# Single tiles of the first expert layer: tokens as the stationary operand, weights as the moving one, and the hidden rows turned back

## The chip, the cores and the metric

The kernel runs on one core of a Trainium2 chip. The metric is the device time of one execution in microseconds (us), the median of three runs. A core has a matrix engine (PE; its weight loads are listed apart, as PEld), a vector engine (DVE), a scalar engine (ACT), a general engine (POOL), which here also issues the indirect transfers, and a queue engine (SP) for plain transfers. A matrix instruction multiplies a stationary operand of 128 x 128, loaded by a weight load ahead of it, with a moving operand of 128 rows and up to 512 columns, and sums into PSUM, which has eight banks of 128 x 512 float32.

## What is computed

Sixteen images and sixteen texts become 165 tokens of 256 numbers each. Two layers follow, each of attention or a scan and then experts. The change lies in the experts of the first layer:

```python
macro_scores = jax.nn.sigmoid(xf @ macro_w)          # 4 groups, the best one is taken
micro_scores = jax.nn.sigmoid(jnp.einsum('td,gde->tge', xf, micro_w))   # both experts of the group
w = (macro_full[:, :, None] * micro_full).reshape(T, NUM_EXPERTS)
gate = jax.nn.silu(jnp.einsum('td,edf->tef', xf, gate_w))   # 256 -> 512
up = jnp.einsum('td,edf->tef', xf, up_w)
h = gate * up
out = jnp.einsum('te,tef,efd->td', w, h, down_w)            # 512 -> 256
```

Each token goes to one group of four, and through both experts of that group. The kernel computes these products in pairs of float16: an operand is split into a high and a low half, and three products (high x high, high x low, low x high) stand for one in float32.

## The kernel before

Tokens are sorted by group into 24 tiles of 128 rows (`SLOT0`). The first 20 tiles form ten pairs, worked on two at a time, with 256 token columns; the last four are worked on singly (`SINGLES0 = 4`), with 128. A pair or a single is a unit: units 0 to 9 are pairs, 10 to 13 singles. `pipelined` (L145) writes units 0 and 1, a hardware loop over units 2 to 7, and then units 8 to 13 one by one. A function of this kind writes each engine's own list of steps; each engine runs its list strictly in order, and semaphores hold it where it needs another engine.

On PE, `tile` (L861) writes for each unit: the products of the unit's first expert (`products_in`, s = 0, in two halves of 256 hidden columns), the transposes of the next unit's token rows (`transpose_x`), the output product of the unit before through its second expert (`product_out(i - 1, 1)`), the products of the second expert (s = 1), and the output product of the first (`product_out(i, 0)`). In `products_in` (L839) a 128 x 128 piece of the weights is stationary and the tokens, held transposed, move; so the hidden rows come out with the hidden index on the partitions, which is what `product_out` (L852) needs for its stationary operand. Its moving operand is 256 columns of the output weights. For a single tile `products_in` issues 24 matrix instructions of 128 columns for a half, 96 for a unit, and `product_out` 12 of 256 columns for an expert. The expert's place in the weights is a register value, read at the start of each unit by `weights` (L857).

Between them ACT applies Silu to the gate (L906) and writes the high half of the scaled hidden rows (L911), and DVE multiplies by `up` (L955) and writes the low half (L960). This goes in four steps per unit, `b` = 0 to 3. The input products use PSUM banks 0 to 3, the outputs banks 4 and 5 (`Y_BANKS`), the token transposes bank 7. ACT then scales the first expert's output (`first_y`, L919), DVE adds the second's (`whole_y`, L969), and POOL sends the rows with an indirect transfer that adds to a sum in device memory (L1017). When all are sent, SP loads that sum back (L1258), DVE takes its statistics, and the attention of the second layer begins; PE meanwhile prepares that layer's routing weights (`prepare_logits`, L1484 and after), and fills waits there with idle products on ones (`keep_clock`, L550).

Far ahead of this, SP loads the expert weights in twelve pieces (L1996), the first ten with a semaphore each and the last two with one between them, and ACT and POOL split them (L2185, L2050).

Of the kernel before, what the change touches and what calls it, by code (L numbers as in the profile page):

```python
# [17 lines left out]
P = 128  # L18
# [116 lines left out]

C_BANKS = (0, 1)
Y_BANKS = (4, 5)

def tile_rows(t):
# [16 lines left out]
def known(i, value):  # L158

    return isinstance(i, int) and i == value  # L160
# [18 lines left out]
def build(nc, txt, patches, wtok, cols, rows_a, consts, pe_table, wsmall, w0, wattn, rows_f, w1, wsmall1,  # L179
          b2rows, out):  # L180
    with ExitStack() as ctx:
# [3 lines left out]
        def sem(name):  # L185
            return ctx.enter_context(nc.semaphore(name))
# [206 lines left out]
        d_moved = sem("d_moved")  # L393
        own_high = sem("own_high")
        w0_split = sem("w0_split")
        w0_loaded = [sem(f"w0_loaded{i}") for i in range(XW // CW // 2 - 1)]

        def w0_landed(m):

            last = len(w0_loaded) - 1  # L400
            return (w0_loaded[m], 16) if m < last else (w0_loaded[last], 32)
        consts_ready = sem("consts_ready")
        rows_known = sem("rows_known")
        dve_done = sem("dve_done")
# [37 lines left out]
        act_out = sem("act_out")  # L442
        h_ready = sem("h_ready")
        y_half = sem("y_half")
        hT_hi = sem("hT_hi")
        hT_lo = sem("hT_lo")
        y_done = sem("y_done")
# [206 lines left out]
        def moved0(slot, tiles):  # L654

            return 16 * len([t for t in range(tiles) if unit0(t) % 2 == slot])

        def landed0(i, slot, j):
            return moved0(slot, first0(i) + 1) if single0(i) else 32 * (j + 1)

# [155 lines left out]
        def pe_experts0(pe):  # L816
            def transpose_x(i, slot, j):
                pe.wait_ge(x_in[slot], landed0(i, slot, j))
                for k in range(KC):
                    for a in range(tiles0(i)):  # L820
                        ins = nc.tensor.transpose(PS[:, 7, (2 * k + a) * P:(2 * k + a + 1) * P],  # L821
                                                  xin[:, slot, a, k * P:(k + 1) * P], k_ident)
                ins.then_inc(x_tr, 1)

            def products_in(i, s, half, w_, slot):

                b = 2 * s + half
                if b == 0:
                    pe.wait_ge(x_lo, i + 1)
                if not (known(i, 0) and s == 0):  # L830
                    pe.wait_ge(h_ready, 4 * i + b - 1)
                tokens = P * tiles0(i)
                for u, done in ((0, gate_psum), (1, up_psum)):
                    for c in range(2):
                        n = 0
                        for k in range(KC):
                            off = in_w0(s * W0N + (u * KC + k) * F0 + (2 * half + c) * P)
                            for x_, at_ in ((xh, off), (xl, off), (xh, off + CW)):
                                ins = nc.tensor.matmul(PS[:, 2 * u + half, c * T1:c * T1 + tokens], w_[:, at_:at_ + P],  # L839
                                                       x_[:, slot, k, 0:tokens], start=(n == 0), stop=(n == 3 * KC - 1))  # L840
                                n += 1
                    ins.then_inc(done, 1)

            def product_out(i, s, w_):

                pe.wait_ge(hT_lo, 4 * i + 2 * s + 2)
                wait_from(pe, y_copied if s else y_begun, first0(i))
                for a in range(tiles0(i)):
                    for c in range(F0 // P):
                        off = in_w0(s * W0N + 2 * KC * F0 + c * D)  # L850
                        for n, (h_, at_) in enumerate(((hTh, off), (hTh, off + CW), (hTl, off))):
                            ins = nc.tensor.matmul(PS[:, Y_BANKS[s], a * D:(a + 1) * D], h_[:, s, c, a * P:(a + 1) * P],  # L852
                                                   w_[:, at_:at_ + D], start=(c == 0 and n == 0),
                                                   stop=(c == F0 // P - 1 and n == 2))
                ins.then_inc(y_done if s else y_half, 1)

            def weights(i):  # L857
                return expert_weights(w0x, 2 * E0 * W0N, slot_expert(pe, first0(i), G0))
            held = [None, None]

            def tile(i, slot, j):  # L861
                w_ = weights(i)
                if known(i, 0):
                    transpose_x(0, 0, 0)
                    keep_clock(18, 6)
                products_in(i, 0, 0, w_, slot)
                products_in(i, 0, 1, w_, slot)
                if not known(i, 0):

                    last = held[1] if slot == 1 or isinstance(i, int) and held[0] == i - 1 else weights(i - 1)  # L870
                if not known(i, UNITS0 - 1):
                    transpose_x(i + 1, 1 - slot, j + slot)
                if not known(i, 0):
                    product_out(i - 1, 1, last)
                products_in(i, 1, 0, w_, slot)
                products_in(i, 1, 1, w_, slot)
                product_out(i, 0, w_)
                held[:] = [i if isinstance(i, int) else None, w_]
            pipelined(pe, UNITS0, tile, SINGLES0)
            product_out(UNITS0 - 1, 1, weights(UNITS0 - 1))  # L880

        def x0_parts(i, half, slot):

# [3 lines left out]

        def h0_parts(i, b):

            s, half = b // 2, b % 2  # L890
            views = (PS[:, half, :].rearrange("p (c r) -> p c r", c=2), PS[:, 2 + half, :].rearrange("p (c r) -> p c r", c=2),
                     sg[:, half], hh[:, half], hTh[:, s, 2 * half:2 * half + 2], hTl[:, s, 2 * half:2 * half + 2])
            if single0(i):
                return (v[:, :, 0:P] for v in views)
            return (v.rearrange("p c r -> p (c r)") for v in views)

        def act_experts0(act):
# [3 lines left out]
                nc.scalar.activation(to, from_, ACT.Copy).then_inc(x_hi, 1)  # L901

            def nonlinear(i, b):
                act.wait_ge(gate_psum, 4 * i + b + 1)
                gate, _, to, _, _, _ = h0_parts(i, b)
                nc.scalar.activation(to, gate, ACT.Silu).then_inc(act_out, 1)  # L906

            def split_h(i, b):
                act.wait_ge(h_ready, 4 * i + b + 1)
                _, _, _, whole, to, _ = h0_parts(i, b)  # L910
                nc.scalar.activation(to, whole, ACT.Copy, scale=hscale[:, 0:1]).then_inc(hT_hi, 1)  # L911

            def first_y(i, slot, j):
# [4 lines left out]
                for a in range(tiles0(i)):  # L918
                    nc.scalar.activation(ybuf[:, slot, a, :], PS[:, Y_BANKS[0], a * D:(a + 1) * D], ACT.Copy,  # L919
                                         scale=wall[:, bass.ds(first0(i) + a, 1), 0]).then_inc(y_begun, 1)  # L920

            def tile(i, slot, j):
                if known(i, 0):
                    split_x(0, 0)
                    act.wait_ge(scale_ready, 1)
                else:
                    first_y(i - 1, 1 - slot, j + slot - 1)
                for b in range(4):
                    nonlinear(i, b)
                    split_h(i, b)  # L930
                    if b == 1 and not known(i, UNITS0 - 1):
                        split_x(i + 1, 1 - slot)
            pipelined(act, UNITS0, tile, SINGLES0)
            first_y(UNITS0 - 1, (UNITS0 - 1) % 2, (UNITS0 - 1) // 2)

        def dve_experts0(dve, chain):
# [12 lines left out]

            def combine(i, b):  # L950

                dve.wait_ge(up_psum, 4 * i + b + 1)
                dve.wait_ge(act_out, 4 * i + b + 1)
                _, up, gate, whole, _, _ = h0_parts(i, b)
                nc.vector.tensor_tensor(whole, up, gate, ALU.mult).then_inc(h_ready, 1)  # L955

            def split_h(i, b):
                dve.wait_ge(hT_hi, 4 * i + b + 1)
                _, _, _, whole, high, low = h0_parts(i, b)
                nc.vector.scalar_tensor_tensor(out=low, in0=whole, scalar=hscale[:, 0:1], in1=high, op0=ALU.mult,  # L960
                                               op1=ALU.subtract).then_inc(hT_lo, 1)

            def whole_y(i, slot):

                dve.wait_ge(y_done, i + 1)
                for a in range(tiles0(i)):
# [3 lines left out]
                                                   scalar=wall[:, bass.ds(first0(i) + a, 1), 1], in1=part, op0=ALU.mult,  # L970
                                                   op1=ALU.add).then_inc(y_copied, 1)

            def tile(i, slot, j):
                if known(i, 0):
                    split_x(0, 0)
                    row_weights(0, 0, 0)
                for b in range(4):
                    combine(i, b)
                    split_h(i, b)
                    if b == 1:  # L980
                        if not known(i, UNITS0 - 1):
                            split_x(i + 1, 1 - slot)
                            row_weights(i + 1, 1 - slot, j + slot)
                        if not known(i, 0):
                            whole_y(i - 1, 1 - slot)
            pipelined(dve, UNITS0, tile, SINGLES0)
            whole_y(UNITS0 - 1, (UNITS0 - 1) % 2)

        def pool_slots(pool, tiles, lag, gather, send):
# [1731 lines left out]
```

## Time and profile before

| | |
|---|---|
| three runs, median (lowest to highest) | 790.91 us (790.46 to 791.1) |
| profiled execution, its own time | 791.43 us |
| its span, first to last instruction | 789.6 us |
| PE busy | 719.4 us, 91% of the span |
| DVE, ACT, POOL busy | 468.2, 375.5, 356.6 us |
| mean granted clock of PE | 0.966 |

The first expert layer runs from about 146 to 352 us of the span, its four single units from about 305 us. In the timeline each line is a run of like instructions on one engine: its start, how long it lasted, engine, line of the kernel, operation, output and inputs, and the count after an x; a bracket at the end is the idle time ahead of it and what ended it. Since matrix instructions overlap, the distance from the start of one group to the start of the next on PE tells what the group took of PE.

### The profile page before, as it was taken

The numbers are of one execution on the slowest core, as the hardware profiler recorded it, in microseconds if no ns is written. First come the engines' busy times: TensorE is split into PE (matmuls) and PEld (weight loads), VectorE is DVE, ScalarE is ACT, GpSimd is POOL, SyncE is SP. The second block draws the span as 40 slices with busy tenths as digits, with TensorE's granted clock in tenths as the row PEclk, the third lists the DMA queues.
The fourth block names the chain that finished last, engine by engine and source line by source line (L and its number), as shares of the span: only waits on it lengthen the run. The fifth ranks groups of instructions, "written<-read, shape, count | busy, mean of one in ns | idle before, by whom it ended". The sixth has DMA issues, their size and how long they took to land.

```text
span 789.6 us, 19052 instructions
## 1 busy us (share of the span) xinstructions
PE 719.4 (91%) x6285; PEld 632.7 (80%) x6286; DVE 468.2 (59%) x1241; ACT 375.5 (48%) x887; POOL 356.6 (45%) x310
## 2 busy tenths in 40 slices
PE   5989983899999999998798997989999999999991
PEld 4768973888888898778688986868888888888871
DVE  4998678444444444337888888945455454554540
ACT  5797657343333343334465665533444434434430
POOL 2539980322233223211676871043665555655331
PEclk9999995999999999999999999999999999999996
DMA  9970044114122111117121334411322233222225
GB/s 270 411 306 2 1 148 148 49 28 117 28 32 41 33 22 29 22 21 226 57 81 54 85 97 159 145 52 38 55 44 47 43 54 54 46 48 41 40 35 150
DMA packets 37192, 66.25 MB, mean 84 GB/s; under 512 B 3776, under 2 KB 29360, under 8 KB 35568
## 3 DMA queue, kind: packets, MB, share of 16 engines
q1 hardware_dynamic: 23696, 46.90, 17.7%
q0 software_dynamic: 13248, 18.21, 14.4%
q8 instruction: 37, 0.61, 0.3%
q10 hardware_dynamic: 192, 0.38, 0.1%
q14 instruction: 19, 0.16, 0.1%
HBM read 44.83 MB, written 23.35 MB: 86 GB/s over the span
## 4 chain that ended last, share of the span: by engine, by line
PE 67%; DVE 15%; POOL 8%; DMA 3%; ACT 3%; issue 2%; POOLq 0%; SPq 0%; DVEq 0%; ACTq 0%
PE PS L839 17%; PE PS L1046 15%; PE PS L1059 15%; PE PS L852 8%; POOL X L2050 6%; PE PS L1419 3%; PE PS L1446 1%; PE PS L1031 1%; DMA Y<-in_wtok_dram 1%; PE PS L1427 1%; POOL X L1671 1%; POOL X L2045 1%; PE PS L821 1%; DVE stats L2467 1%; DVE rs L2400 1%
## 5 line engine op out<-in xcount | busy, mean ns | idle before, releaser
L839 PE MATMUL PS<-Y,X 128*128 128x256 f16 (+1 forms) x1344 | 139.0, 258 | 1.6 <-issue 0.9
L839 PEld LDWEIGHTS PS<-Y,X 128*128 x1344 | 119.4, 98 | 18.2 <-issue 3.1
L1225 POOL DMA_INDIRECT sum<-X,dest x45 | 88.8, 1973 | 96.6 <-ACT X L1128 81.4
L1059 PE MATMUL PS<-X 128*128 x720 | 125.7, 273 | 2.0 <-ACT X L1128 1.9
L1046 PE MATMUL PS<-X 128*128 128x256 f16 (+1 forms) x768 | 122.6, 265 | 0.4 <-issue 0.4
L1118 ACT ACTIVATE X<-PS,X 128x256 f32<-128x256 f32 (+1 forms) x192 | 72.6, 461 | 103.3 <-PE PS L1046 100.2
L1046 PE MATMUL PS<-X,Y 128*128 128x256 f16 (+1 forms) x384 | 100.2, 264 | 0.0
L1059 PE MATMUL PS<-Y,X 128*128 x360 | 98.2, 273 | 0.0
L1017 POOL DMA_INDIRECT sum<-Y,dest x24 | 38.7, 1611 | 116.1 <-DVE Y L969 112.8
L1046 PEld LDWEIGHTS PS<-X 128*128 x768 | 71.8, 97 | 10.3 <-issue 0.9
L1059 PEld LDWEIGHTS PS<-X 128*128 128x128 f16 x720 | 70.4, 98 | 11.1 <-issue 3.1
L955 DVE TENSOR_TENSOR Y<-PS,Y 128x512 f32<-128x512 f32 (+1 forms) x56 | 34.4, 615 | 68.8 <-PE PS L839 65.2
L1211 POOL DMA_INDIRECT X<-xs,source x45 | 45.7, 1015 | 65.2 <-DVE source L750 33.0
L911 ACT ACTIVATE Y<-Y,hscale 128x512 f16<-128x512 f32 (+1 forms) x56 | 37.0, 660 | 72.3 <-DVE Y L955 72.3
L852 PE MATMUL PS<-X,Y 128*128 x576 | 67.6, 273 | 0.4 <-DVE Y L960 0.3
L1177 DVE SCALAR_TENSOR_TENSOR PS<-PS,hscale,X 128x256 f32<-128x256 f32 x45 | 20.0, 488 | 74.8 <-PE PS L1059 74.8
L960 DVE SCALAR_TENSOR_TENSOR Y<-Y,hscale 128x512 f16<-128x512 f32 (+1 forms) x56 | 38.1, 680 | 40.8 <-ACT Y L911 40.8
L852 PEld LDWEIGHTS PS<-X,Y 128*128 128x128 f16 x576 | 55.6, 98 | 7.9 <-issue 0.8
L1169 DVE SCALAR_TENSOR_TENSOR X<-X,hscale 128x1024 f16<-128x1024 f32 (+1 forms) x48 | 58.5, 1218 | 1.7
L2050 POOL TENSOR_TENSOR X<-X 128x256 f16<-128x256 f32 (+1 forms) x55 | 58.2, 1092 | 0.5
L1007 POOL DMA_INDIRECT Y<-xs,source x24 | 23.7, 989 | 59.4 <-DVE Y L947 29.8
L906 ACT ACTIVATE Y<-PS 128x512 f32<-128x512 f32 (+1 forms) x56 | 29.6, 528 | 32.9 <-PE PS L839 32.4
(402 smaller groups left out, 1389.6 us busy)
## 6 DMA issues: line engine op xcount, KB each, us to landing
X<-in_w_dram SPq DMA_DIRECT2D x11, 1024.0 KB, 16.1
stage<-in_w_dram SPq DMA_DIRECT2D x16, 512.0 KB, 3.5
sum<-h SPq DMA_DIRECT2D x2, 2048.0 KB, 7.5
xs<-Y SPq DMA_DIRECT2D x2, 1040.0 KB, 5.4
xs<-Y SPq DMA_DIRECT2D x2, 1032.0 KB, 5.1
h<-in_txt_dram SPq DMA_DIRECT2D x2, 1024.0 KB, 17.3
Y<-in_patches_dram SPq DMA_DIRECT2D x3, 672.0 KB, 8.2
sum<-h SPq DMA_DIRECT2D x2, 768.0 KB, 6.4
```

Of the source, the lines that this page charges most:

```text
L839: ins = nc.tensor.matmul(PS[:, 2 * u + half, c * T1:c * T1 + tokens], w_[:, at_:at_ + P], x_[:, slot, k, 0:tokens], start=(n == 0), stop=( ...
L852: ins = nc.tensor.matmul(PS[:, Y_BANKS[s], a * D:(a + 1) * D], h_[:, s, c, a * P:(a + 1) * P], w_[:, at_:at_ + D], start=(c == 0 and n == ...
L911: nc.scalar.activation(to, whole, ACT.Copy, scale=hscale[:, 0:1]).then_inc(hT_hi, 1)
L960: nc.vector.scalar_tensor_tensor(out=low, in0=whole, scalar=hscale[:, 0:1], in1=high, op0=ALU.mult, op1=ALU.subtract).then_inc(hT_lo, 1)
L1017: nc.gpsimd.indirect_dma_start(out=sum0, out_offset=bass.IndirectOffsetOnAxis(ap=dest[:, i:i + 1], axis=0), in_=ybuf[:, u % 2, i - first0( ...
L1046: ins = nc.tensor.matmul(PS[:, 2 * s + c // 2, (c % 2) * T1:(c % 2) * T1 + tokens], part[:, off:off + P], x_[:, slot, k, 0:tokens], start= ...
L1059: ins = nc.tensor.matmul(PS[:, 4 + a, 0:D], h_[:, s, c, a * P:(a + 1) * P], part[:, off:off + D], start=(s == 0 and c == 0 and n == 0), st ...
L1118: ins = nc.scalar.activation(hh1[:, s, c, 0:tokens], PS[:, 2 * s + c // 2, (c % 2) * T1:(c % 2) * T1 + tokens], ACT.Gelu, bias=bias1[:, sl ...
L1169: nc.vector.scalar_tensor_tensor(out=lo_, in0=act_, scalar=hscale[:, 2:3], in1=hi_, op0=ALU.mult, op1=ALU.subtract).then_inc(h1_lo, 1)
L1211: nc.gpsimd.indirect_dma_start(out=x1in[:, u % 2, n - first_tile(u), :], out_offset=None, in_=xs1, in_offset=bass.IndirectOffsetOnAxis(ap= ...
L1225: nc.gpsimd.indirect_dma_start(out=sum1, out_offset=bass.IndirectOffsetOnAxis(ap=dest[:, i:i + 1], axis=0), in_=y1buf[:, u % 2, i - first_ ...
L2050: ins = nc.gpsimd.tensor_tensor(w0_low(n)[:, of], w0_landing(n)[:, of], w0_high(n)[:, of], ALU.subtract)
```

## The change

Pairs are left as they are. In a single unit the operands of the input products change places: a 128 x 128 piece of the tokens is stationary, and 512 columns of weights move, so one instruction fills a whole bank with the gate (or up) rows of one expert. That makes 12 instructions for an expert and 24 for a unit, in place of 96. The hidden rows now come out with the tokens on the partitions, and Silu and the product with `up` run on 128 x 512 in one step per expert instead of two of 128 x 256. They then have to be turned back: `transpose_h` sends four 128 x 128 float32 transposes through PE into one further bank (`TURN_BANK = 6`), from which ACT and DVE write the high and the low halves. That bank is held until DVE has written the low half. The order in a single unit is written anew on PE, ACT and DVE; `product_out(i, 0)` moves from the end of unit `i` into the next unit, and the last unit's rest follows behind the loop. One semaphore is added for the turned rows, and one is taken from the weight loads, so that the last three pieces share one and all three must land before any of them is split.

```diff
-Y_BANKS = (4, 5)
+Y_BANKS, TURN_BANK = (4, 5), 6
...
-        w0_loaded = [sem(f"w0_loaded{i}") for i in range(XW // CW // 2 - 1)]
+        w0_loaded = [sem(f"w0_loaded{i}") for i in range(XW // CW // 2 - 2)]
...
-            return (w0_loaded[m], 16) if m < last else (w0_loaded[last], 32)
+            return (w0_loaded[m], 16) if m < last else (w0_loaded[last], 48)
...
+            def single_in(i, s, w_, slot):
+                if s == 0:
+                    pe.wait_ge(x_lo, i + 1)
+                pe.wait_ge(h_ready, step0(i, s) - 2)
+                for u, done in ((0, gate_psum), (1, up_psum)):
+                    n = 0
+                    for k in range(KC):
+                        off = in_w0(s * W0N + (u * KC + k) * F0)
+                        for x_, at_ in ((xh, off), (xh, off + CW), (xl, off)):
+                            ins = nc.tensor.matmul(PS[:, 2 * u + s, 0:F0], x_[:, slot, k, 0:P], w_[:, at_:at_ + F0],
+                                                   start=(n == 0), stop=(n == 3 * KC - 1))
+                            n += 1
+                    ins.then_inc(done, 1)
+            def transpose_h(i, s):
+                pe.wait_ge(h_ready, step0(i, s))
+                pe.wait_ge(hT_lo, step0(i, s) - 1)
+                for c in range(F0 // P):
+                    ins = nc.tensor.transpose(PS[:, TURN_BANK, c * P:(c + 1) * P],
+                                              hh[:, s].rearrange("p c r -> p (c r)")[:, c * P:(c + 1) * P], k_ident)
+                ins.then_inc(hT_psum, 1)
...
             def product_out(i, s, w_):
-                pe.wait_ge(hT_lo, 4 * i + 2 * s + 2)
+                pe.wait_ge(hT_lo, step0(i, s) if single0(i) else step0(i, 2 * s + 1))
...
+            def single(i, slot, j):                       # PE
+                w_ = weights(i)
+                after = single0(i - 1)
+                single_in(i, 0, w_, slot)
+                if after:
+                    transpose_h(i - 1, 1)
+                if not known(i, UNITS0 - 1):
+                    transpose_x(i + 1, 1 - slot, j + slot)
+                product_out(i - 1, 0 if after else 1, held[1])
+                single_in(i, 1, w_, slot)
+                transpose_h(i, 0)
+                if after:
+                    product_out(i - 1, 1, held[1])
+                held[:] = [i, w_]
...
-            product_out(UNITS0 - 1, 1, weights(UNITS0 - 1))
+            product_out(UNITS0 - 1, 0, held[1])
+            transpose_h(UNITS0 - 1, 1)
+            product_out(UNITS0 - 1, 1, held[1])
...
+            def single(i, slot, j):                       # ACT
+                after = single0(i - 1)
+                if not after:
+                    first_y(i - 1, 1 - slot, j + slot - 1)
+                nonlinear(i, 0)
+                if after:
+                    split_h(i - 1, 1)
+                if not known(i, UNITS0 - 1):
+                    split_x(i + 1, 1 - slot)
+                if after:
+                    first_y(i - 1, 1 - slot, j + slot - 1)
+                nonlinear(i, 1)
+                split_h(i, 0)
...
+            split_h(UNITS0 - 1, 1)
             first_y(UNITS0 - 1, (UNITS0 - 1) % 2, (UNITS0 - 1) // 2)
...
+            def single(i, slot, j):                       # DVE
+                after = single0(i - 1)
+                combine(i, 0)
+                if after:
+                    split_h(i - 1, 1)
+                if not known(i, UNITS0 - 1):
+                    split_x(i + 1, 1 - slot)
+                    row_weights(i + 1, 1 - slot, j + slot)
+                if not after:
+                    whole_y(i - 1, 1 - slot)
+                combine(i, 1)
+                split_h(i, 0)
+                if after:
+                    whole_y(i - 1, 1 - slot)
...
+            split_h(UNITS0 - 1, 1)
             whole_y(UNITS0 - 1, (UNITS0 - 1) % 2)
```

## Rows read from the trace of the kernel before

**Rows 1.** The page's part 4: the chain that ended last, by engine.
```profile
PE 67%; DVE 15%; POOL 8%; DMA 3%; ACT 3%; issue 2%; POOLq 0%; SPq 0%; DVEq 0%; ACTq 0%
```

**Rows 2.** The chain in order of time: start us, us, what held the end.
```profile
297.20 5.24 PE PS L839 x48
...
351.58 0.50 DVE Y L969
...
352.34 4.49 DMA sum<-Y,dest
...
356.89 2.86 DMA h<-sum
...
363.19 0.34 DVE X L1717
```

**Rows 3.** Timeline of PE over the single units and what follows.
```profile
304.90 3.20 PE L839 MATMUL PS<-Y,X 128*128 128x128 f16 x48
307.94 0.39 PE L821 MATMUL PS<-cst,Y 128*128 128x128 f32 x2
308.16 2.78 PE L852 MATMUL PS<-X,Y 128*128 x24
...
315.45 4.29 PE L839 MATMUL PS<-Y,X 128*128 128x128 f16 x48 [0.31 <-issue]
...
321.15 3.96 PE L839 MATMUL PS<-Y,X 128*128 128x128 f16 x48
325.15 1.50 PE L852 MATMUL PS<-X,Y 128*128 x12
326.91 4.45 PE L839 MATMUL PS<-Y,X 128*128 128x128 f16 x48 [0.26 <-issue]
...
350.04 1.50 PE L852 MATMUL PS<-X,Y 128*128 x12 [0.33 <-DVE Y L960]
351.38 1.04 PE L1484 MATMUL PS<-cst,Y 128*128 128x128 f32 x8
352.34 1.05 PE L1488 MATMUL PS<-onesf,wsm 1*128 1x1 f32 x8
```

**Rows 4.** PE groups by form: busy us, mean ns of one; idle before.
```profile
L839 PE MATMUL PS<-Y,X 128*128 128x128 f16 x384 | 30.9, 223 | 1.1 <-issue 0.9
```

**Rows 5.** Last weight load's issue, landing times of all twelve, a late split on ACT.
```profile
46.62 0.43 SPq L1996 DMA_DIRECT2D stage<-in_w_dram  x1
...
DMA to landing us min/median/max: 5.3/15.1/26.1
...
101.45 1.06 ACT L2185 ACTIVATE X<-X 128x1024 f16<-128x1024 f32 x1 [0.30 <-POOL X L2050]
```

**Rows 6.** DVE and ACT on 128 x 512, by form, and two DVE starts.
```profile
L955 DVE TENSOR_TENSOR Y<-PS,Y 128x512 f32<-128x512 f32 x40 | 27.6, 691 | 51.9 <-PE PS L839 48.3 <-ACT Y L906 3.6
L960 DVE SCALAR_TENSOR_TENSOR Y<-Y,hscale 128x512 f16<-128x512 f32 x40 | 30.4, 759 | 31.6 <-ACT Y L911 31.6
L901 ACT ACTIVATE Y<-PS 128x512 f16<-128x512 f32 x10 | 5.8, 579 | 9.6 <-PE PS L821 9.6
...
299.86 0.69 DVE L955 TENSOR_TENSOR Y<-PS,Y 128x512 f32<-128x512 f32 x1 [1.74 <-PE PS L839]
349.25 0.49 DVE L960 SCALAR_TENSOR_TENSOR Y<-Y,hscale 128x256 f16<-128x256 f32 x1 [0.58 <-ACT Y L911]
```

**Rows 7.** PE after idle time, and a stretch with its granted clock (PEclk).
```profile
52.75 1.37 PE L2295 MATMUL PS<-cst,Y 128*128 128x128 f32 x8 [1.39 <-DVE Y L2513]
357.82 2.02 PE L1502 MATMUL PS<-Y,X 128*128 128x260 f32 x8 [1.08 <-ACT wsm L1617]
363.66 0.66 PE L1390 MATMUL PS<-cst,X 128*128 128x128 f32 x2 [0.93 <-DVE X L1717]
...
391.37 0.69 PE L1407 MATMUL PS<-cst,X 128*128 128x128 f32 x2 [3.43 <-ACT X L2074]
...
core 0: us, PE busy (x), PEclk, DMA share, GB/s
52.00:54.00 2.00, 1.14 (x9) 1.00 1.05 442
364.00:366.00 2.00, 2.00 (x14) 0.50 0.98 330
```

More of the change, by code:

```diff
@@ L444, in build @@
         y_half = sem("y_half")
+        hT_psum = sem("hT_psum")
         hT_hi = sem("hT_hi")
@@ L656, in moved0, with step0, alone0 @@
             return 16 * len([t for t in range(tiles) if unit0(t) % 2 == slot])
+        def step0(i, b):
+            return 4 * PAIRS0 + 2 * (i - PAIRS0) + b + 1 if single0(i) else 4 * i + b + 1
+        def alone0(i, s):
+            return 2 * (i - PAIRS0) + s + 1
         def landed0(i, slot, j):
@@ L859, in pe_experts0 @@
             held = [None, None]
+            def single(i, slot, j):
[12 more added lines that the diff above has]
+                held[:] = [i, w_]
             def tile(i, slot, j):
+                if single0(i):
+                    single(i, slot, j)
+                    return
                 w_ = weights(i)
@@ L888, in h0_parts @@
         def h0_parts(i, b):
+            if single0(i):
+                turned = PS[:, TURN_BANK, :].rearrange("p (c r) -> p c r", c=F0 // P)
+                return (PS[:, b, :], PS[:, 2 + b, :], sg[:, b].rearrange("p c r -> p (c r)"), hh[:, b].rearrange("p c r -> p (c r)"),
+                        turned, hTh[:, b, :, 0:P], hTl[:, b, :, 0:P])
             s, half = b // 2, b % 2
             views = (PS[:, half, :].rearrange("p (c r) -> p c r", c=2), PS[:, 2 + half, :].rearrange("p (c r) -> p c r", c=2),
-                     sg[:, half], hh[:, half], hTh[:, s, 2 * half:2 * half + 2], hTl[:, s, 2 * half:2 * half + 2])
-            if single0(i):
-                return (v[:, :, 0:P] for v in views)
+                     sg[:, half], hh[:, half], hh[:, half], hTh[:, s, 2 * half:2 * half + 2], hTl[:, s, 2 * half:2 * half + 2])
             return (v.rearrange("p c r -> p (c r)") for v in views)
@@ L903, in nonlinear @@
             def nonlinear(i, b):
-                act.wait_ge(gate_psum, 4 * i + b + 1)
-                gate, _, to, _, _, _ = h0_parts(i, b)
+                act.wait_ge(gate_psum, step0(i, b))
+                gate, _, to, _, _, _, _ = h0_parts(i, b)
                 nc.scalar.activation(to, gate, ACT.Silu).then_inc(act_out, 1)
             def split_h(i, b):
-                act.wait_ge(h_ready, 4 * i + b + 1)
-                _, _, _, whole, to, _ = h0_parts(i, b)
+                if single0(i):
+                    act.wait_ge(hT_psum, alone0(i, b))
+                else:
+                    act.wait_ge(h_ready, step0(i, b))
+                _, _, _, _, whole, to, _ = h0_parts(i, b)
                 nc.scalar.activation(to, whole, ACT.Copy, scale=hscale[:, 0:1]).then_inc(hT_hi, 1)
@@ L920, in first_y @@
                                          scale=wall[:, bass.ds(first0(i) + a, 1), 0]).then_inc(y_begun, 1)
+            def single(i, slot, j):
[11 more added lines that the diff above has]
+                split_h(i, 0)
             def tile(i, slot, j):
+                if single0(i):
+                    single(i, slot, j)
+                    return
                 if known(i, 0):
@@ L950, in combine @@
             def combine(i, b):
-                dve.wait_ge(up_psum, 4 * i + b + 1)
-                dve.wait_ge(act_out, 4 * i + b + 1)
-                _, up, gate, whole, _, _ = h0_parts(i, b)
+                dve.wait_ge(up_psum, step0(i, b))
+                dve.wait_ge(act_out, step0(i, b))
+                _, up, gate, whole, _, _, _ = h0_parts(i, b)
                 nc.vector.tensor_tensor(whole, up, gate, ALU.mult).then_inc(h_ready, 1)
             def split_h(i, b):
-                dve.wait_ge(hT_hi, 4 * i + b + 1)
-                _, _, _, whole, high, low = h0_parts(i, b)
+                dve.wait_ge(hT_hi, step0(i, b))
+                _, _, _, _, whole, high, low = h0_parts(i, b)
                 nc.vector.scalar_tensor_tensor(out=low, in0=whole, scalar=hscale[:, 0:1], in1=high, op0=ALU.mult,
@@ L971, in whole_y @@
                                                    op1=ALU.add).then_inc(y_copied, 1)
+            def single(i, slot, j):
[12 more added lines that the diff above has]
+                    whole_y(i - 1, 1 - slot)
             def tile(i, slot, j):
+                if single0(i):
+                    single(i, slot, j)
+                    return
                 if known(i, 0):
```

## The prediction

> **What bounds the kernel now.** I read the page's part on the chain that ended last first: PE holds 67% of it, no other engine more than 15% [rows 1]. What matters is whether PE holds it where the change is made. The chain in order of time says so: through the expert layer it consists of input products (L839) and output products (L852), one behind the other, without a pause between pairs; behind the last single unit it passes to DVE's last addition, to POOL's last indirect transfer, to SP's load of the sum, and by DVE's norm back to PE [rows 2]. So a microsecond taken from PE before the last output product is a microsecond off the end, as long as nothing on that line is late for a reason of its own, and everything behind it moves along.
>
> Then the timeline of PE. The reader should compare pitches there, that is the distance of group starts over the count, not durations, since instructions overlap. In a pair 48 products of 256 columns take 5.24 us [rows 2], 109 ns each. In the singles 48 products of 128 columns should take half; the first unit comes near that, 48 in 3.04 us (304.90 to 307.94) or 63 ns each. But the next units take 4.00 us (321.15 to 325.15), 83 ns each, and lose more at their starts: 12 output products alone take 1.34 us (350.04 to 351.38), yet the next unit begins 1.76 us after they do (325.15 to 326.91), with idle time that ends by "issue", so with no other engine to blame [rows 3]. A single unit takes 11.46 us (315.45 to 326.91). By columns it should take 96 x 55 ns + 2 x 1.34 + 0.22, some 8.2 us. PE is thus bound by getting its many short instructions and weight loads out, not by columns. All 384 of them are busy for 30.9 us [rows 4].
>
> **The change part by part.** *Input products.* The columns stay: 96 x 128 per unit are now 24 x 512. No 512-column product stands in the trace; the nearest are the float16 products of 256 columns, which also read one operand at a register's address, at 109 ns. Twice that is 218 ns, 2.62 us for the 12 of one expert. Bounds: no gain per column against the singles as they are, 4 x 83 = 333 ns; below, 213 ns, a column per cycle of 2.4 GHz, which 109 ns for 256 columns come close to. I take 218, since only the column count differs. The weight load of the next piece of tokens lies beside 218 ns of streaming, as it does beside 109 in a pair.
>
> The Trainium skill ("TensorE: Matmul & The Clock Gate", Back-to-back issue gap) gives a sustained 131 ns for products of 512 columns with their loads, and 216 alone; the pairs' 109 ns for half the columns speaks for the second. By the first the 96 products would take 8.4 us less than I reckon.
>
> *Turning back.* Eight times four float32 transposes. The trace has the same kind at 0.96 us for 8 (351.38 to 352.34) and 0.22 for 2 [rows 3]: 0.12 each, 0.48 for a turn. Bounds 0.11 and 0.20 (the 0.39 that two last by themselves), that is -0.3 to +2.6 us over 32; I take 0.12, as they follow one another.
>
> *Output products* stay: 1.34 us for 12, 24 x 109 ns = 2.62 for those of the last pair. *Token transposes* stay: 0.22.
>
> *Sum on PE, with nothing late.* Unit 10: 2.62 in + 0.22 + 2.62 out of pair 9 + 2.62 in + 0.48 = 8.56. Units 11 and 12: 2.62 + 0.48 + 0.22 + 1.34 + 2.62 + 0.48 + 1.34 = 9.10 each. So unit 13 begins at 304.90 + 8.56 + 18.20 = 331.66.
>
> *The new waits.* In unit 11 or 12, from its start: input products end at 2.62 and 7.28, turns at 3.10 and 7.76, output products run from 3.32 and 7.76. DVE began 0.20 after the pitch end of its products (297.04 + 2.62 against 299.86); on 128 x 512 DVE takes 0.69 for the product and 0.76 for the low half, ACT 0.58 out of PSUM [rows 6]. So the first expert's hidden rows are there at 3.51 and are turned from 7.28; the rows turned at 3.10 have their low half at about 4.7, and the next turn, which needs their bank, comes at 7.28, their output product at 7.76; the rows turned at 7.76 are split by 9.3, while the next turn is at 11.7 and the output product at 12.4. The smallest margin is over 2 us. PE has behind each of these waits all it has left, so a late split would cost in full, but none is late. ACT waits for the turn with the next tokens' split and the first output behind it; these end at about 5.3, and the next unit's products need the tokens at 9.10. POOL's sends come 9 us apart and land 4.5 us after they start [rows 2], and its gathers need only the token transposes, which stay early.
>
> *The tail is where it costs.* Unit 13 has no token transposes. Its last turn in the loop ends at 7.54 from its start, the output product of unit 12 at 8.88. ACT 7.74 to 8.32, DVE 8.34 to 9.10, and PE starts 0.30 after DVE (349.74 to 350.04, [rows 3, 6]): 9.40, so PE idles 0.5. Output product to 10.74, turn to 11.22, ACT 11.42 to 12.00, DVE 12.02 to 12.78, PE at 13.08 after 1.9 us of waiting with nothing to put there. Before, no turn stood in this line. Last output product: 331.66 + 13.08 = 344.74, against 350.04. The gain is 5.3 us. It would be some 7.7 without the two waits.
>
> *The rest.* The last three weight loads share a semaphore. The last is issued at 46.62 and at the longest landing seen, 26.1 us, is there by 73; the first chunk that newly waits is split on ACT at 101.45, held by POOL [rows 5]. Cost nothing, cover 28 us. The last unit's register load at the end falls away: hidden already.
>
> The profiled execution: 789.6 - 5.3 = 784.3 of span, with the same 1.8 us around it 786.1. The median of the runs lies 0.5 lower than that execution's time, so 790.91 - 5.3 = **785.6 us**. The start gaps of units 11 to 13 (0.42 each, 1.3 us in all) I count as gone, because PE now streams 218 ns per instruction, and the issuing gets ahead as it does in pairs; if they stay, 786.9.
>
> **The rivals.**
> *The tail lets the clock fall.* Idle of 1.39 us (52.75) left the clock at 1.00; 3.43 us ahead of 391.37 and the pair of 1.08 and 0.93 ahead of 363.66 were followed by 0.50, the 1.2 GHz level [rows 7]. The tail has 0.5 and 1.9 within four microseconds, between. Then the last 12 output products take 1.3 us more, and the preparation behind them, at half speed, some 0.3 to 1 more than its cover: 787.2 to 787.9. Against it: dense work just before. A fall that moves behind the layer can also spare the one at 364, up to 2 us the other way.
> The Trainium skill (the same page, PE-mode transpose) says that transposes don't keep the clock up as products do; here four of them stand between 12 products each, and the eight of L1484 ran without a fall.
> *PE waits for the turned rows in each unit*, because ACT or DVE are later than reckoned: from 2 us of lateness on, each step adds. Three units at 1.2 us: 789.2. Against it the margins above.
> *The wide products stream no cheaper* than four short ones: slower. Place: all 96. At 333 ns they cost 96 x 115 = 11.0 us more than reckoned, 796.6. It decides from 218 + 5300/96 = 273 ns on. For it: the singles' own rate per column; against it: the pairs' 109 ns.
> *Wide products overlap*, so that 512 columns take hardly longer than 256. At 109 ns they cost 96 x 109 = 10.5 us less: 775.1. Against it: in the pairs and the first single unit time goes with columns. The Trainium skill's 131 ns above belongs here and would give 777.2.
>
> **How the numbers follow.** Forecast 0.71, with its own range 784.0 to 787.0; clock in the tail 0.14; waits in each unit 0.07; wide products slow 0.06; overlap 0.02. What a measurement here can tell from no change is 0.2%, 1.6 us: 789.3 to 792.5. Faster: 0.71 + 0.14 + 0.02 and half of the waits, 0.90. Same: the other half and a mild case of slow products, 0.05. Slower 0.05. The range runs from 783.0 (the cheapest bounds, -0.8 us, and the fall at 364 spared) to 789.3 (waits), and leaves out the slow products and the overlap.
>
> **What would show it.** In the changed trace 12 products of 512 columns should take 2.6 us by their starts and a unit 9.1; four turns 0.5; PE idle only twice, 0.5 and 1.9 us, ahead of the last two output products; the last of them should begin at about 344.7 and the sum's load at about 351.6. A unit at over 10.5 us with PE idle "DVE L960" says waits; the same without idle says slow products; 0.50 in the clock from 343 to 348 says the tail. If the load of the sum comes 5 us earlier and the end does not, the prediction is wrong behind the layer.

## The result, and the profile after

The changed kernel takes 784.16 us (median of four runs, 783.53 to 784.72) against 791.0 in the same comparison: ratio 0.9913, 95% interval 0.9902 to 0.9925. Forecast were 785.6 and a range of 783.0 to 789.3. The profiled execution took 783.53 us with a span of 781.7; before, 791.43 and 789.6. Now and then a run of a kernel, changed or not, takes some 10 us more than its others.

In the changed kernel's lines, L862 are the wide input products, L872 the turn, L884 the output products, L829 the token transposes, L968 and L1035 the high and low halves on ACT and DVE, L1578 the first step behind the layer. First its timeline of PE (start us, us, engine, line, operands, count, idle before), which answers to [rows 3]:

```profile
303.99 2.75 PE L862 MATMUL PS<-X,Y 128*128 x12
306.58 0.38 PE L829 MATMUL PS<-cst,Y 128*128 128x128 f32 x2
...
312.01 0.60 PE L872 MATMUL PS<-cst,Y 128*128 128x128 f32 x4
312.45 2.75 PE L862 MATMUL PS<-X,Y 128*128 x12
315.04 0.60 PE L872 MATMUL PS<-cst,Y 128*128 128x128 f32 x4
315.47 0.38 PE L829 MATMUL PS<-cst,Y 128*128 128x128 f32 x2
315.69 1.47 PE L884 MATMUL PS<-X,Y 128*128 x12
317.00 2.75 PE L862 MATMUL PS<-X,Y 128*128 x12
319.59 0.60 PE L872 MATMUL PS<-cst,Y 128*128 128x128 f32 x4
320.03 1.47 PE L884 MATMUL PS<-X,Y 128*128 x12
321.34 2.75 PE L862 MATMUL PS<-X,Y 128*128 x12
...
337.59 1.47 PE L884 MATMUL PS<-X,Y 128*128 x12
339.40 1.50 PE L884 MATMUL PS<-X,Y 128*128 x12 [0.34 <-DVE Y L1035]
340.74 0.60 PE L872 MATMUL PS<-cst,Y 128*128 128x128 f32 x4
342.99 1.50 PE L884 MATMUL PS<-X,Y 128*128 x12 [1.65 <-DVE Y L1035]
344.32 1.04 PE L1578 MATMUL PS<-cst,Y 128*128 128x128 f32 x8
```

The reader sees a unit without a bracket, that is without idle time: from 312.45 to 321.34 PE goes from group to group, 8.89 us, where a unit took 11.46 [rows 3]. The starts that had idle time by "issue" have none. Only the last two output products wait, for DVE, 0.34 and 1.65 us. From the start of the singles to the last output product it is 342.99 - 303.99 = 39.00 us; before, 350.04 - 304.90 = 45.14. The change itself gives 6.14 us in this pair of traces.

By form (busy us, mean ns of one | idle before), against the 30.9 us of [rows 4]:

```profile
L862 PE MATMUL PS<-X,Y 128*128 x96 | 22.0, 379 | 0.0
```

The rest of the 7.9 us between the spans is not shown to be of the change's making. The singles begin 0.91 us earlier, and so does the whole layer: its first token transposes start at 143.10 against 144.01. In the profiles of the other runs but one the singles begin anywhere from 303.43 to 304.78. Behind the layer the chain of waits is this (start us, us, what; compare [rows 2]):

```profile
342.99 1.50 PE PS L884 x12
...
350.76 2.76 PE PS L1596 x8
353.52 1.73 PE PS L1599 x4
...
357.00 0.38 ACT wsm L1714
357.38 0.08 ACT wsm L1715
...
357.50 0.44 PE PS L1484 x2
```

Before, it passed over the last transfer, the load of the sum and DVE's norm; now it passes over PE's and ACT's preparation of the routing weights, which has become the later of the two. Two things differ on the way there. The last transfer was quicker, 3.74 us from POOL's start to the next load against 4.55 (from 352.34 to 356.89 in [rows 2]):

```profile
345.28 1.55 POOL L1111 DMA_INDIRECT sum<-Y,dest  x1 [3.80 <-DVE Y L1044]
...
349.02 2.80 SPq L1352 DMA_DIRECT2D h<-sum  x5
```

And the clock fell during the preparation instead of behind it (window, length and PE busy, clock; 0.50 is 1.2 GHz), so that L1596 took 2.76 us against 2.02 before [rows 7], and L1599 1.73 against 1.04:

```profile
core 0: us, PE busy (x), PEclk, DMA share, GB/s
342.00:344.00 2.00, 1.01 (x10) 1.00 0.55 66
352.00:354.00 2.00, 2.00 (x6) 0.50 0.95 257
384.00:386.00 2.00, 1.92 (x12) 1.00 0.00 0
```

It is the clock that made the preparation the later one: in the profiles of the experiments e2, e4 and e7 below the transfer was as quick (3.78 to 3.87 us) and the clock stayed up there, and PE waited for DVE's norm again, by 0.8 us. The third row shows the other side: PE idles 3.42 us ahead of 384.08, as it did 3.43 us ahead of 391.37, but the clock stays up this time. Such falls move attention's length from profile to profile. From the load of the sum to the next layer's first store it was 123.8 us before, 122.9 here, and 122.9 to 124.5 in the profiles of the experiments.

### The profile page after: what moved, and what is told of

The parts are those of the page before. It is cut to its first block, busy times and chain, and to the rows that moved or that the text cites. A ratio compares the mean times of both kernels' runs of the same rounds, so it can differ in the third digit from the quotient of the medians.

```text
span 781.7 us, 18313 instructions
## 1 busy us (share of the span) xinstructions
PE 711.0 (91%) x6029; PEld 619.4 (79%) x6030; DVE 465.2 (60%) x1225; ACT 371.6 (48%) x871; POOL 356.5 (46%) x310
## 4 chain that ended last, share of the span: by engine, by line
PE 67%; DVE 15%; POOL 8%; ACT 4%; issue 2%; DMA 1%; POOLq 0%; SPq 0%; DVEq 0%; ACTq 0%
PE PS L1140 15%; PE PS L1153 15%; PE PS L847 13%; PE PS L884 8%; POOL X L2144 6%; PE PS L1513 3%; PE PS L862 3%; PE PS L1540 1%; PE PS L1125 1%; PE PS L1521 1%; POOL X L2139 1%; POOL X L1765 1%; DMA ccols<-in_cols_dram 1%; PE PS L829 1%; DVE rs L2494 1%
## 5 line engine op out<-in xcount | busy, mean ns | idle before, releaser
L847 PE MATMUL PS<-Y,X 128*128 128x256 f16 x960 | 108.1, 273 | 0.5 <-DVE Y L1016 0.5
L847 PEld LDWEIGHTS PS<-Y,X 128*128 x960 | 93.9, 98 | 11.5 <-issue 0.7
L1030 DVE TENSOR_TENSOR Y<-PS,Y 128x512 f32<-128x512 f32 x48 | 33.2, 692 | 68.5 <-PE PS L847 48.3
L884 PE MATMUL PS<-X,Y 128*128 x576 | 67.5, 273 | 2.0 <-DVE Y L1035 2.0
L884 PEld LDWEIGHTS PS<-X,Y 128*128 128x128 f16 x576 | 56.2, 98 | 8.9 <-issue 2.5
L968 ACT ACTIVATE Y<-Y,hscale 128x512 f16<-128x512 f32 x40 | 28.9, 722 | 55.7 <-DVE Y L1030 55.7
L1035 DVE SCALAR_TENSOR_TENSOR Y<-Y,hscale 128x512 f16<-128x512 f32 x40 | 30.4, 759 | 31.6 <-ACT Y L968 31.6
L960 ACT ACTIVATE Y<-PS 128x512 f32<-128x512 f32 x48 | 28.3, 589 | 35.8 <-PE PS L847 24.9
```

## Experiments

The theories in short. Mine: a short product costs PE what its issuing costs, a longer one its columns, so the gain comes from fewer and wider products; and a turn needs other work of PE as cover. The rivals: the new order of steps, the fewer steps on ACT and DVE, or the full bank made the gain.

**Half as wide: e1_w256.**

```diff
+WIDE = 256
...
+                    for c in range(0, F0, WIDE):
...
-                            ins = nc.tensor.matmul(PS[:, 2 * u + s, 0:F0], x_[:, slot, k, 0:P], w_[:, at_:at_ + F0],
...
+                                ins = nc.tensor.matmul(PS[:, 2 * u + s, c:c + WIDE], x_[:, slot, k, 0:P], w_[:, at_:at_ + WIDE],
```

> The changed kernel with its wide input products cut in two: 256 weight columns each, 24 per expert, the rest as changed. My theory (a short product costs what its issuing costs, a longer one its columns): at 256 columns the columns still decide, 109 ns each as in the pairs, 2.62 us per expert against 2.59, so 784.2 to 785.0. Rival (what helps is that one instruction fills a whole bank): part of the gain is lost, 786 or more.

Measured: 784.86 us, ratio to before 0.9895 (0.9827 to 0.9963). The timeline of PE, last output product at the end:

```profile
304.33 2.78 PE L864 MATMUL PS<-X,Y 128*128 x24
306.95 0.38 PE L830 MATMUL PS<-cst,Y 128*128 128x128 f32 x2
...
343.57 1.52 PE L886 MATMUL PS<-X,Y 128*128 x12 [1.65 <-DVE Y L1037]
```

24 take 2.62 us (304.33 to 306.95), and the stretch from the singles' start to the last output product 39.24 us against 39.00. A full bank per instruction is worth 0.03 us per expert and no more.

**A quarter as wide: e2_w128.** The same edit with `WIDE = 128`.

> The changed kernel with its wide input products cut in four: 128 weight columns each, 48 per expert, which is as many products of as many columns as before the change, but with the tokens stationary, the new order of steps and the fewer steps on ACT and DVE. My theory (issuing bounds short products): 83 ns each again, 4.0 us per expert instead of 2.59, eight times 1.4 = 11 us more, so 794 to 796, and PE idle by issue between units again. Rival (the new order, or the fewer steps on the other engines, made the gain): 784 to 786.

Measured: 794.28 us, ratio 1.0048 (1.0005 to 1.009). PE's timeline, and the group's products by form:

```profile
303.87 3.26 PE L864 MATMUL PS<-X,Y 128*128 x48
306.96 0.39 PE L830 MATMUL PS<-cst,Y 128*128 128x128 f32 x2
...
313.64 4.28 PE L864 MATMUL PS<-X,Y 128*128 x48 [0.47 <-DVE Y L1032]
317.77 0.63 PE L874 MATMUL PS<-cst,Y 128*128 128x128 f32 x4
...
352.89 1.50 PE L886 MATMUL PS<-X,Y 128*128 x12 [1.65 <-DVE Y L1037]
```

```profile
L864 PE MATMUL PS<-X,Y 128*128 x384 | 30.6, 223 | 0.6 <-DVE Y L1032 0.5
```

In the first single unit 48 take 3.09 us and less, in the later ones between 3.48 and 4.35 (4.13 from 313.64 to 317.77), so 72 to 91 ns each there; 83 were expected. All 384 are busy for 30.6 us, where they were busy for 30.9 before the change [rows 4]. The stretch to the last output product is 352.89 - 303.87 = 49.02 us, 10 more than in the changed kernel and 3.9 more than before the change. So with 128 columns the stationary operand, the order and the fewer steps elsewhere do not even make up for the turns: the gain needs the width. One point was missed: PE does not idle by "issue" between units again. One unit's start waited for DVE, 0.47 us, and two more came some 0.2 us late.

**What makes a short product slow: e3_static.** The kernel before, with the input products of single units at a fixed address; the hidden rows of single tiles are then those of one group.

```diff
-                products_in(i, 0, 0, w_, slot)
...
+                w_in = w0x[:, 0:2 * E0 * W0N] if single0(i) else w_
+                products_in(i, 0, 0, w_in, slot)
...
```

The other three calls of `products_in` are changed alike.

> The kernel before, with the input products of the four single units reading the weights of one fixed group at a fixed address instead of the group's own by a register (the single tiles' hidden rows are those of that group). My theory, if the register step of 46 ns between the products is what makes issuing slow: 48 products at 56 ns, 2.7 us instead of 4.0 or more, a unit of 8.7 us instead of 11.5, so 781 to 784. If a weight load and a product alone take 83 ns to issue: no change, 791. Rival (single units wait for ACT and DVE): no change either, 791, but with idle time ended by DVE.

Measured: 780.56 us, ratio 0.9874 (0.9791 to 0.9956). Its timeline of PE and its products by form:

```profile
311.64 1.47 PE L852 MATMUL PS<-X,Y 128*128 x12
312.95 2.84 PE L839 MATMUL PS<-Y,X 128*128 128x128 f16 x48
315.63 0.39 PE L821 MATMUL PS<-cst,Y 128*128 128x128 f32 x2
...
337.93 1.50 PE L852 MATMUL PS<-X,Y 128*128 x12 [0.42 <-DVE Y L961]
```

```profile
L839 PE MATMUL PS<-Y,X 128*128 128x128 f16 x384 | 22.7, 219 | 0.0
```

48 take 2.68 us (312.95 to 315.63), 56 ns each: the same 128-column products, the same number of weight loads, the same waits, and 8.2 us less busy time. A unit takes 8.20 us (312.95 to 321.15). Gaps at unit starts are gone too: 311.64 + 1.31 is 312.95.
```profile
L839 PEldq FUSED_REGOPS  x247: 46/46/46, 304.9 to 347.9; - x124
```

```profile
L864 PEldq FUSED_REGOPS  x256: 46/46/46, 302.7 to 346.7; - x128
```

Two thirds of 46 is 31 ns; with 56 that makes an estimate of 87, and 83 to 90 is what the products took in units 11 to 13 before the change. That the step simply adds to the 56 ns is not shown beyond this. In the first single unit they took 57 to 64 ns in both kernels in spite of the step; there the queue still had a lead (in e2 its first steps begin at 302.7, the first product at 303.87), while the last step begins at 346.7 and the last product at 346.9. At 256 columns, 109 ns, the step fits beside the columns. So "issue" was mainly this step. The run also bounds what is left: were the weights at a known address, the old arrangement would need no turn, and its stretch from the singles' start to the last output product is 34.50 us (303.43 to 337.93) where the change takes 39.00. By the medians, of separate jobs, the end is 3.6 us earlier, but e3's four runs spread over 11 us.

**The tail: e4_tail.** The last unit's second turn goes to bank 7, which holds nothing by then, and stands ahead of the last two output products.

```diff
-                pe.wait_ge(hT_lo, step0(i, s) - 1)
+                pe.wait_ge(hT_lo, step0(i, s) - (2 if last_turn(i, s) else 1))
...
-                    ins = nc.tensor.transpose(PS[:, TURN_BANK, c * P:(c + 1) * P],
+                    ins = nc.tensor.transpose(PS[:, 7 if last_turn(i, s) else TURN_BANK, c * P:(c + 1) * P],
...
+            transpose_h(UNITS0 - 1, 1)
             product_out(UNITS0 - 1, 0, held[1])
-            transpose_h(UNITS0 - 1, 1)
             product_out(UNITS0 - 1, 1, held[1])
```

> The changed kernel with one thing moved: the last unit's second turn goes to bank 7, which is free by then, and stands ahead of the last two output products, in PE's wait for the rows turned before. My theory (the two waits of the tail are on the path): the last output product begins 1.8 us earlier, at 341.2 instead of 343.0, and the end comes 1.8 us earlier, 782.4; with less idle time the clock may also stay up at 352, up to 1 us more. Rival (what follows is held by the preparation of the routing weights or by the transfers anyway): 784.

Measured: 783.21 us, ratio 0.9881 (0.9829 to 0.9933), between the 782.4 of the theory and the 784 of the rival.

```profile
337.72 1.47 PE L887 MATMUL PS<-X,Y 128*128 x12
339.03 0.60 PE L875 MATMUL PS<-cst,Y 128*128 128x128 f32 x4
339.53 1.50 PE L887 MATMUL PS<-X,Y 128*128 x12
341.28 1.50 PE L887 MATMUL PS<-X,Y 128*128 x12 [0.25 <-DVE Y L1038]
```

The turn fills the first wait, and the second shrinks from 1.65 to 0.25 us; the last output product begins at 341.28 instead of 342.99. That part is shown. What of the 1.7 us reaches the end, the next runs try.

**The moved step put back: e5_order.**

```diff
-                product_out(i - 1, 0 if after else 1, held[1])
+                if not after:
+                    product_out(i - 1, 1, held[1])
                 single_in(i, 1, w_, slot)
                 transpose_h(i, 0)
+                product_out(i, 0, w_)
...
-            product_out(UNITS0 - 1, 0, held[1])
```

> The changed kernel with the moved step put back: product_out(i, 0) stands at the end of unit i again, right behind the turn of its rows, instead of behind the next unit's first input products. My theory (a turn needs cover, since its way over ACT and DVE takes 1.65 us, as the tail shows): PE idles 1.65 us in each of the units 10 to 13, where it idled 0, 0, 0 and 0.34, so 6.3 us more than the changed kernel, 790 to 791, no better than before. Rival (the queue of PE covers it, or the order does not matter): 784 to 785.

Measured: 792.56 us, ratio 1.002 (1.0008 to 1.0032).

```profile
312.54 0.60 PE L872 MATMUL PS<-cst,Y 128*128 128x128 f32 x4
314.79 1.50 PE L884 MATMUL PS<-X,Y 128*128 x12 [1.65 <-DVE Y L1036]
316.57 2.76 PE L862 MATMUL PS<-X,Y 128*128 x12 [0.28 <-issue]
...
324.67 2.81 PE L884 MATMUL PS<-X,Y 128*128 x24 [1.65 <-DVE Y L1036]
...
351.51 1.50 PE L884 MATMUL PS<-X,Y 128*128 x12 [1.65 <-DVE Y L1036]
```

Each turn without cover costs 1.65 us of idle PE, and the whole gain goes: from the start of the singles at 304.52 to the last output product it is 46.99 us, 7.99 more than in the changed kernel. It went further than I expected, by the gaps at the starts of units: 12 products from 314.79 end their share of PE at 316.12, but the next begin at 316.57. Such gaps, 0.3 to 0.45 us, stand at the start of each of three units. The likely cause is that behind a wait PE's queue has no lead, so that the register read at a unit's start shows again; the read itself stands there in e3 too, where it costs nothing that shows.

**The changed kernel and the tail in one job: e6_after_again, e7_tail_again.**

> The changed kernel as it is, on the same chip as the next two, to compare with: 784.2, and 6 to 7 us under the kernel before.

> The changed kernel with the last unit's second turn in bank 7, ahead of the last two output products (as e4_tail). My theory: 1.7 us under the changed kernel in the same job, as the last output product began 1.7 us earlier in its trace. Rival (lost behind the layer): within 0.5 us of it.

Measured: 784.26 us, ratio 0.9916 (0.9896 to 0.9936), and 782.65 us, ratio 0.9907 (0.9878 to 0.9937). The medians differ by 1.6 us, as expected, and the earlier jobs agree (784.16 and 783.21). But runs of one kernel spread by some 3 us there and more, and the intervals overlap: the tail's gain is shown in the layer, likely at the end, and not proven there. In the traces of these two, the loads of the sum lie 2.0 us apart and the next layer's first stores only 0.8, since from load to store it took 122.9 us in e6 and 124.1 in e7.

**Waits behind the layer filled: e8_tail_clock.**

```diff
+                keep_clock(17, 7)
                 pe.wait_ge(prep_copied, 3)
...
-                keep_clock(15, 7)
+                keep_clock(28, 7)
                 pe.wait_ge(prep_copied, 4)
```

> As e7_tail_again, and idle products on ones put in two waits of PE behind the layer, 17 more in the wait of 1.08 us ahead of L1596 of the changed kernel and 13 more behind L1603. If the fall of the clock around 352 to 358 us comes from these waits and costs what it covers: no fall there, and up to 1.5 us less than e7, 781. Rival (the fall is beside the path of the transfers, or moves to the next wait): within 0.5 us of e7.

Measured: 784.29 us (780.9 to 792.89), ratio 0.9901 (0.988 to 0.9922); 781 was expected. Without the longest run of each kernel the medians are 783.5 here and 782.6 for e7: no gain. In its one profile, of the run at 792.89 us, the clock reads 1.00 from 350 to 368 us. But e7's profile reads 1.00 there too, without the filling, so in this pair there was no fall to remove, and whether the filling helps where the clock falls is left open.

## Why the prediction was right

The mechanism held in the layer, step by step; behind it the time agreed in part for other reasons, and there the agreement was partly luck.

*What bounds the singles*: PE's issuing, shown by e3, which removes it without touching width, order or steps, and by e2, which brings it back in the new arrangement. The prediction named "many short instructions and weight loads"; that was too wide, since e3 keeps their number and takes 8.20 us for a unit, the 8.2 that the prediction reckoned by columns. What is slow is the register step.

*Input products*: 2.62 us per expert were reckoned from twice the pairs' 109 ns; 2.59 were measured (303.99 to 306.58). The slow wide products did not come, nor did the overlap. By the Trainium skill's sustained 131 ns for 512 columns ("TensorE: Matmul & The Clock Gate", Back-to-back issue gap) the 12 would take an estimated 1.6 us, which this trace does not bear out. Its 216 ns for one alone is what 2.59 us over 12 gives.

*Turns*: 0.48 reckoned, 0.44 measured (312.01 to 312.45), the lower bound. *Output products*: 1.31, not 1.34. A unit is 8.89, not 9.10.

*The new waits*: none in the units, as the margins said; e5 shows what they cover. *The tail*: 0.5 and 1.9 us were reckoned from where the group ahead ends by its pitch. Counted alike, 0.50 and 1.81 were measured (from 338.90 to 339.40 and from 341.18 to 342.99); the brackets' 0.34 and 1.65 count from the end of the last instruction. Two errors nearly cancel in it: ACT took 0.69 us and not 0.58, and PE started 0.13 us after DVE and not 0.30:

```profile
341.38 0.69 ACT Y L968
342.07 0.03 issue
342.10 0.76 DVE Y L1035
342.86 0.13 issue
342.99 1.50 PE PS L884 x12
```

These terms, each a little too dear, make the difference in the layer: 5.3 us forecast, 6.14 measured. The input products give 0.24 of it, the turns some 0.3, the output products 0.2. *The gaps at unit starts* went, as counted. *The shared semaphore* of the last weight loads cost nothing that shows: the layer begins 0.91 us earlier, not later.

*The rest*, 6.84 us by the medians against 6.14 in the layer, is not assigned. That the last transfer lands quicker (3.74 us against 4.55) was not forecast. In the seven other profiles with tokens stationary it took 3.6 to 3.9, in the one other of the old arrangement (e3) 5.4; why was not tried.

*Everything behind moves along*: here the number held better than the reasoning. In the pair of traces the load of the sum comes 7.87 us earlier (349.02 against 356.89), and the end 7.9. Between them, PE's first step of attention comes only 6.16 us earlier (357.50 against 363.66), because the slowed preparation held it. Attention then gives that back, and some more, where the clock stays up: 9.25 us to DVE's next step on the chain against 10.35, and 10.32 against 11.77 around the long idle. The first of these gains was named under the clock's rival, the second was luck. By the next layer's first store the lead is 8.75 us (471.94 against 480.69), of which the span keeps 7.9.

*The clock*: it did not fall in the tail, whose idle is 2.0 us of some 4, and the eight turns between the products left it at 1.00 from 300 to 350. It fell at 352, in the preparation, behind a further 1.08 us; the rival had the fall at the tail itself. Whether the tail has a part in it stays open. Of the five profiles with the tail's waits (the changed kernel, e1, e2, e5 and e6) four show the fall in the preparation, all but e2; of the two kernels with the shorter tail e4 shows one only at 354, behind the preparation, and e7, the same kernel, none there. That points to the tail; so few profiles do not show it.

## What to carry to other kernels

Before a short matrix product is counted by its columns, look at what PE's queue runs between products: a weight piece at a register's address costs a step of 46 ns, which hides beside 256 columns and not beside 128. Making the register-addressed operand the moving one, and wide, buys that back, and a turn of the result costs 0.44 us as long as other products stand between the turn and its use; without that cover it cost 1.65 us more here. At the end of a layer little cover is left, so the last turn should be issued into a spare bank as early as its rows allow: that brought the last output product 1.7 us forward.

## What was not expected of the hardware

The same idle of PE, 3.42 and 3.43 us at the same place of attention, was followed by the lower clock in one trace and not in the other; between the projections on both sides of it 11.77 us passed with the fall (384.56 to 396.33) and 10.32 without it (377.29 to 387.61). The ten profiles of this case all have this idle time, 3.42 or 3.43 us long; the lower clock followed in seven and not in three (the changed kernel, e5 and e6). What decides is not shown. One profile therefore cannot settle a difference of a microsecond at the end.
